# The stacks of a fused attention and convolution kernel: six transfers in a row, or three pairs that wait for TensorE's progress

## The reference

```python
# layer 0: shifted-window attention (windows of 8 x 8, shift 4, 3 heads of 8), then a gated convolution
xn  = layernorm(x over channels);  xw = windows(roll(xn, -4, -4))
q, k, v = split(xw @ qkv_w.T + qkv_b)
attn = softmax(q * hd**-0.5 @ k.T + bias + mask);  out = attn @ v @ proj_w.T + proj_b
x = x + roll(unwindow(out), 4, 4)
y = layernorm(x over channels, tokens in order).reshape(B, C, H, W)   # token rows read back as channel planes
y = conv3x3_depthwise(pin_w @ y)                                     # 24 -> 126 channels
x = x + pout_w @ (gelu(y[:, :63]) * y[:, 63:])
# layer 1: h = bn(w1 x); h = [h, max over even shifts of h - roll(h)]; gelu, two 1x1 products, residual, MLP
```

## Time and profile before

| what | value |
|---|---|
| three runs | 231.26 us median, 230.91 to 235.5 |
| profiled execution | 230.8 us, of which the span from first to last instruction is 228.9 |
| mean granted TensorE clock | 0.993 |
| busy share of the span | PE 92%, DVE 70%, ACT 60%, POOL 56% |
| transfers on SyncE's and the other hardware queue | 23.16 MB, 33.6% of 16 engines' span |
| instruction packets on queue q8 | 29, 0.48 MB |
| landing of store_y's 144 KB transfers, median | 2.3 us from issue |

### The profile page before, as it was taken

The page is one execution under the profiler, slowest core; times in us unless marked ns, Lnnn a source line. Parts: engine busy times, 40 slices in busy tenths (PEclk is TensorE's granted clock), DMA queues, the critical chain, the costliest instruction groups (busy, mean ns, idle before and its releaser), DMA issues.

```text
span 228.9 us, 8584 instructions
## 1 busy us (share of the span) xinstructions
PE 210.9 (92%) x3634; PEld 109.6 (48%) x3634; DVE 159.3 (70%) x284; ACT 137.0 (60%) x226; POOL 127.1 (56%) x165
## 2 busy tenths in 40 slices
PE   7779899999999999997799999999999987999980
PEld 4346666676757667665455444443333311222240
DVE  4677969698997989798755756344368789655332
ACT  3567676777859686763236333333346774898980
POOL 8245948466988869695989993223320000245433
PEclk9999999999999999999999999999999999999997
DMA  6950000120130464665637367777400001243312
GB/s 159 307 148 3 3 3 9 37 72 3 39 74 22 106 228 132 200 215 160 196 84 253 113 244 183 232 235 271 153 4 0 4 0 33 64 114 94 82 37 69
DMA packets 12541, 25.09 MB, mean 110 GB/s; under 512 B 6618, under 2 KB 8162, under 8 KB 10775
## 3 DMA queue, kind: packets, MB, share of 16 engines
q1 hardware_dynamic: 11606, 23.16, 33.6%
q0 software_dynamic: 896, 1.38, 2.7%
HBM read 18.63 MB, written 3.15 MB: 95 GB/s over the span
## 4 chain that ended last, share of the span: by engine, by line
PE 82%; DVE 7%; issue 4%; POOL 2%; ACT 2%; DMA 1%; POOLq 0%; DVEq 0%
PE psum L668 13%; PE psum L669 12%; PE psum L613 10%; PE psum L624 7%; PE psum L642 7%; PE psum L859 4%; PE psum L659 4%; PE psum L573 3%; PE psum L839 3%; PE psum L569 3%; PE psum L817 3%; PE psum L830 2%; PE psum L596 2%; PE psum L580 2%; PE psum L588 2%
## 5 line engine op out<-in xcount | busy, mean ns | idle before, releaser
L505 POOL TENSOR_TENSOR diff<-biased,mx 128x768 f32<-128x768 f32 x31 | 45.7, 1475 | 22.7 <-DVE mx L1146 22.7
L1277 DVE TENSOR_TENSOR gated<-psum,gel 64x512 f32<-64x512 f32 x32 | 22.1, 693 | 24.5 <-ACT gel L1030 24.5
L324 POOL DMA_DIRECT2D out<-yo x28 | 14.2, 515 | 44.2 <-DVE yo L1379 44.2
L1142 DVE TENSOR_TENSOR biased<-psum,pk 128x768 f32<-128x768 f32 x31 | 29.5, 952 | 11.2 <-PE psum L613 10.9
L1030 ACT ACTIVATE gel<-psum 64x512 f32<-64x512 f32 x32 | 18.9, 591 | 30.7 <-PE psum L669 30.6
L954 ACT ACTIVATE pt<-psum 128x768 f32<-128x768 f32 x32 | 25.9, 810 | 16.6 <-PE psum L624 16.4
L668 PE MATMUL psum<-sta,pk 108*128 108x512 f32 x64 | 33.7, 608 | 0.5 <-issue 0.5
L669 PE MATMUL psum<-stb,pk 108*128 108x512 f32 x64 | 32.7, 592 | 0.0
L1146 DVE TENSOR_REDUCE mx<-biased 128x12 f32<-128x768 f32 x31 | 29.5, 953 | 1.1
L613 PE MATMUL psum<-kmv,stq 32*64 32x192 f32 x512 | 28.1, 334 | 0.4 <-DVE biased L1154 0.3
L642 PEld LDWEIGHTS psum<-val,pt 128*32 128x32 f32 x1536 | 17.1, 110 | 12.4 <-issue 12.2
(11 more groups left out here) (108 smaller groups left out, 343.9 us busy)
## 6 DMA issues: line engine op xcount, KB each, us to landing
sta<-scratch SPq DMA_DIRECT2D x24, 288.0 KB
stb<-scratch SPq DMA_DIRECT2D x24, 288.0 KB
xtok<-xt SPq DMA_DIRECT2D x8, 192.0 KB, 4.2
xin<-xw SPq DMA_DIRECT2D x8, 192.0 KB, 5.5
x<-x1s SPq DMA_DIRECT2D x28, 48.0 KB
out<-yo POOLq DMA_DIRECT2D x28, 48.0 KB, 2.0
pk<-pack SPq DMA_DIRECT2D x1, 827.5 KB, 7.1
scratch<-ytok SPq DMA_DIRECT2D x4, 192.0 KB, 3.9
```

What stands on the lines that cost most here:

```text
L505: g.tensor_tensor(diff[:, t % 2].rearrange("q g w n -> q (g w) n"), scores_of, mx[:, t % 2].unsqueeze(2).to_broadcast([128, 4 * NH, WT]), ...
L1142: v.tensor_tensor(biased[:, slot].rearrange("q (p s) -> q p s", p=2), banks, wt("rpb").unsqueeze(1).to_broadcast([128, 2, 2 * NH * WT]), A ...
L1277: v.tensor_tensor(gated[64 * (b % 2):64 * (b % 2) + 64, b // 2, c * CH:(c + 1) * CH], bank(u % 4)[64:128], gel[:, u % 4, :], ALU.mult).the ...
```

## The change

load_stack takes a semaphore and two counts in place of the flag that was always off. Its first two transfers go out at once; the third (y = 2 of sta) waits until the semaphore has reached the first count, and with it goes the fourth; the fifth waits for the second count, and with it goes the sixth. For image 0 and image 1's first half the semaphore is mixed, behind them conv_made. Image 2's first half waits for 8 and 9 there, its second half and image 3 for 10 and 10.

```diff
-        def load_stack(queue, b, h, paced=False):
+        def load_stack(queue, b, h, progress, second, third):
...
-                    if paced and (n or y):
-                        at, before = divmod(3 * n + y - 1, 3)
-                        queue.wait_ge(stack_in[at][b][h], 16 * (before + 1))
+                    if 3 * n + y == 2:
+                        queue.wait_ge(progress, second)
+                    if 3 * n + y == 4:
+                        queue.wait_ge(progress, third)
...
-                    load_stack(sp, b, 0, False)
-                if m in (5, 7):
-                    load_stack(sp, m // 2 - 2, 1, False)
+                    load_stack(sp, b, 0, mixed, *((21, 22) if m == 4 else (29, 30)))
+                if m == 5:
+                    load_stack(sp, 0, 1, mixed, 26, 27)
+                if m == 7:
+                    load_stack(sp, 1, 1, conv_made, 3, 4)
             store_y(sp, 5)
             wait_for_y(2)
             sp.wait_ge(scores_made, 4 * NCH)
-            load_stack(sp, 2, 0)
+            load_stack(sp, 2, 0, conv_made, 8, 9)
...
-            load_stack(sp, 2, 1)
+            load_stack(sp, 2, 1, conv_made, 10, 10)
...
-            load_stack(sp, 3, 0)
+            load_stack(sp, 3, 0, conv_made, 10, 10)
             sp.wait_ge(conv_made, NCH)
-            load_stack(sp, 3, 1)
+            load_stack(sp, 3, 1, conv_made, 10, 10)
```

## The result

The changed kernel took 236.75 us (median of four runs, 235.94 to 237.26), the kernel before 231.08 beside it (229.17 to 235.5). The ratio is 1.0256, with a 95% interval from 1.0197 to 1.0314: slower, by about 5.9 us; whether by more than two per cent, of which the prediction speaks, the interval leaves open. Forecast were 233.6 in 230.4 to 236.0, so the direction was right and the time lies 0.75 us above the range. The profiled execution took 236.44 us with a span of 234.6 (230.8 and 228.9 before), and the mean granted clock is 0.983 against 0.993.

A forecast was written before the change was run, and what follows sets the result against it. TensorE's work bounds until about 153, then SyncE's list. Late masks put convolution 24 +2.0 us; with the clock's 1.5 it starts at 163.5 against 160.9, +2.6: 233.4, plus 0.2 gives 233.6, range 230.4 to 236.0.

The forecast's parts named there:

- two per cent, of which the prediction speaks: Whole kernel: 4.6 us, about what a measurement tells from no change; chances faster 0.01, slower 0.09, within 0.90.
- SyncE is 2.1 us later: SyncE's list at image 1's second half: starts at 119.63 instead of 117.55, and the lateness goes on undiminished.
- My bound of +3.5: Upper bound on SyncE's lateness, if image 1's first half takes the 6.2 us that it took before.
- The 1.0 us that the prediction gives these waits: Image 1's second half, waits on conv_made 3 and 4: nothing, or 1.0 us if TensorE is not 2.9 us ahead.
- The second part of the size is the clock: Behind TensorE's 4.5 us stand before convolution 20: clock falls to 0.50, costing 1.5 us, bounded by nothing and 2.9.
- If both gaps close, it reaches convolution 20 at 150.6.: TensorE comes 2.91 us sooner than 153.53, then stands 4.5 us until masks at 155.1.
- the two gaps: TensorE stops in mixes at 103.35 (1.56 us) and 109.33 (1.35), read as running dry of instructions; worth 2.91 us.
- the first rival, the sooner landing: store_y(5) lands 2.3 us after issue, not 6.3, making everything behind 1.9 us sooner; 228.5 to 230.3, chance 0.10.
- Image 0's first half: SyncE's list free some 3 us later at about 89.3; nothing waits there, the next wait swallows the delay.
- "Nothing" for the waits on conv_made: Image 1's second half and image 2: waits over when the list reaches them, so nothing added if TensorE is ahead.
- The slip of residual(7): VectorE's residual(7) needs store_x1(5), issued until 119.6; a slip costs TensorE up to 1 us, taken from its later stand.
- The second rival: Gaps stay or move: 1.56 us stays in mix 27, SyncE 3.7 us late; 234.4 to 236, chance 0.13.

The follow-up runs named there:

- 1: Changed kernel with only the waits of image 0's second half (mixes 26 and 27) kept; 235.32 us, ratio 1.0185 to the kernel before.
- 6: 4 with the waits on conv_made left out, so waits in image 0 alone; 231.5 us, ratio 0.9928 to the kernel before.
- 15: Changed kernel with only the waits on mixes 26 and 27, behind store_y(3) and store_x1(4), and store_y(5) ahead of image 1's second half; 230.21 us, 0.996.
- 4: Changed kernel with store_y(3) and store_x1(4) ahead of image 0's last two second-half pairs, no waits on mixes 29 and 30; 233.76 us, ratio 1.0076.
- 10: Changed kernel with only the waits on conv_made, none on mixed; 234.73 us, ratio 1.0228 to the kernel before.
- 11: Changed kernel with only the waits of image 0's first half (mixes 21 and 22); 231.93 us, ratio 1.0113 to the kernel before.
- 5: Changed kernel plus five extra 512-column multiplications on TensorE ahead of convolution 20; 234.90 us, ratio 1.0111 to the kernel before.
- 12: Changed kernel run once more, nothing altered; 232.73, 236.23, 236.55 and 236.64 us.
- 14: Changed kernel as it is, run beside 13 on one chip; 235.87 us, ratio 1.0207 to the kernel before.
- 3: Changed kernel plus ten extra 512-column multiplications on TensorE ahead of convolution 20; 238.93 us, ratio 1.0319 to the kernel before.
- 8: Kernel before, without added waits, with store_y(5) moved ahead of image 1's second half; 230.83 us, ratio 0.9949.
- 2: Changed kernel with all added waits but those of image 0's second half (mixes 26 and 27); 238.82 us, ratio 1.0302 to the kernel before.
- 13: Changed kernel plus four extra multiplications (3.4 us) on TensorE ahead of convolution 20; 234.43 us, ratio 1.0161 to the kernel before.

## Why the prediction was wrong, point by point

**The mechanism was the one forecast.** The waits of image 0's second half hold SyncE's list, nothing behind absorbs it, TensorE's stand moves to convolution 20, and the clock falls there. Kernels 1, 6 and 15 show it from both sides: two waits alone bring three quarters of the loss, and with the same waits listed behind the stores it is gone. In the three profiles with a late list, nothing added to TensorE and the clock up behind the stand (4, 10, 11), image 2's first half is 2.13, 1.69 and 0.48 us late, and the execution 2.0, 2.1 and 0.5 us longer than that of the kernel before.

**The step that failed is "SyncE is 2.1 us later", the list's term, in its size.** It was 3.95 in the profile. The 1.87 us between come from single pieces: the third pair went out at 104.00, not 103.45 (+0.55: the mix ended at 103.98 instead of 103.38, behind a gap of 0.53 that has appeared at 99.38 in TensorE's list, and SyncE followed after 0.02, not the 0.07 that the sum has); store_y(3) took 1.26 with its pause, not 0.42 (+0.84); store_y(4) 2.42, not 2.01 (+0.41, one issue of 1.17); the rest 0.07. I used for each piece its own row of the trace before and replaced the one long issue in them by the normal row. But both parts of the sum change from one execution to the next. Issues of one to two microseconds come again and again, at other places: from the end of the third pair to image 1's second half the list took 14.73 us in 5, 15.17 in 12, 15.34 in 14, 15.97 in the profile after, 16.16 in 1 and 16.60 in 3, where the sum has 14.60. And the list inherits whatever time TensorE has lost by mix 27: the third pair was out at 104.84 in 14 and at 106.49 in 3, where the sum has 105.03. Together the list was 2.11 us late in 5, 2.63 in 14, 3.95 and 4.01 in the profile after and in 12, and 5.54 in 3. My bound of +3.5 took one long stack for all of them.

**Nor would 2.1 us have lasted.** The sum has TensorE 2.9 us ahead at the waits on conv_made; it was 0.95 ahead at convolution 0. A list near the forecast is then held next by convolution 3: with image 1's second half at 119.66 and 120.18, store_y(5) still went out 3.2 (5) and 3.1 us late (14). The 1.0 us that the prediction gives these waits if TensorE is not ahead is also too little by the chain of the kernel before, where convolution 3 ends at 124.28 + 0.86 = 125.14:

```profile
124.28 0.86 PE psum L669 x2
```

The last pair, two issues of 0.79, would be out at 126.7, 2.3 us after the 124.4 of the sum.

**The second part of the size is the clock:** 2.05 us against the 1.5 taken, inside the bounds; it was 2.9 in 1 and 1.6 in 14. The upper bound came from a row that can't carry it. The granted clock recorded beside the eight matmuls at the kernel's start is 1.00, not 0.50 (window, us, PE busy, clock, DMA share, GB/s; the kernel before), so that their 5.49 us are no price of the lower level:

```profile
3.00:5.00 2.00, 2.00 (x4) 1.00 1.04 266
```

That 2.9 was a good upper bound all the same is luck.

**Why the range failed too.** At convolution 20 the time was 157.75 against 155.1 forecast, +2.65: 1.74 of the list (3.82 late at image 2's second half against 2.08), 0.8 of a stack that landed later still, 0.11 of start. With 0.55 of the clock that is the 3.2 us by which the time missed. Both upper ends stood in the text, but they were not taken together: 153.0 + 3.5 + 6.87 + 2.9 = 166.3, or +5.4 and about 236.4; even that has no term for the stack's later landing. They are not independent either: a later list makes a longer stand, and the clock was down over convolution 20 after stands of 3.10 (1), 4.50 (12) and 4.67 us (the profile after), and up after 1.66 (4), 2.06 (10) and 2.82 (14).

**"If both gaps close, it reaches convolution 20 at 150.6."** Both were gone, and TensorE reached it at 153.08 (before 153.53). Of the 2.91 us, 0.95 were left at convolution 0 (111.81 against 112.76) and 0.45 here; the rest went at the wait for residual(7), below. PE's timeline of the changed kernel shows what came next:

```profile
99.91 0.61 PE L655 MATMUL psum<-pk,ot 128*96 128x128 f32 x4 [0.53 <-issue]
...
106.17 0.59 PE L627 MATMUL psum<-pk,diff 64*128 64x64 f32 x12 [0.32 <-POOL diff L508]
107.10 0.88 PE L616 MATMUL psum<-kmv,stq 32*64 32x192 f32 x16 [0.35 <-DVE biased L1145]
...
109.64 0.59 PE L627 MATMUL psum<-pk,diff 64*128 64x64 f32 x12 [0.47 <-POOL diff L508]
110.66 0.64 PE L655 MATMUL psum<-pk,ot 128*96 128x128 f32 x4 [0.43 <-DVE ot L1176]
```

I read the two gaps as 2.91 us of TensorE's time. POOL and VectorE, both in the chain of each step, were next late after about one: the four waits for them and the new gap of 0.53 are 2.10 us. Nor is the closing of both gaps the change's alone: in 8 and 10, without an added wait in attention, the gap of 1.35 at 109.33 is gone too, and in 10 TensorE comes to convolution 0 at 112.16, 0.60 us ahead. That the stand came out at 4.67 against the 4.5 forecast is an accident: TensorE came 2.5 later than forecast, and the masks 2.5 later as well.

**What held:** store_y(5) landed 6.3 us after its issue (126.27 to 132.55), so the first rival, the sooner landing, fell. Its mechanism exists: the landing took 4.6 us in 2, 4.4 in 4 and 4.1 in 10, where the waits on conv_made hold the stack ahead apart, and 2.9 in 15, where the store stands ahead of the stack. **Image 0's first half** cost 0.5 us in the profile of 11. **"Nothing" for the waits on conv_made** held in the changed kernel, where the list arrives late, and is wrong as a property of those waits (4, 5, 10). **The slip of residual(7)** came as named: it waited for store_x1(5), which is the chain's 2.54 us of transfer at 120.75, and TensorE for it 0.26.

**The second rival** had nearly the right list, 3.7 us late, by a mechanism that was not there: mix 27 ran through in 0.56. It was near by its number only. The page "Runtime: NRT & Kernel Launch" of the Trainium skill, section "Instruction fetch mechanics", calls the crossing of an instruction block "mostly hidden"; kernel 2 shows a crossing that cost 2.53 us with six transfers ahead of it, kernel 11 one at the same place that cost at most 0.3 with the same six, and kernels 6 and 15 show all crossings between 84 and 113 us hidden, with the same transfers spread.

**What stays open.** How much of the time is the clock's: the rows give 2.05 us in the profile after, 2.9 in 1 and 1.6 in 14 (convolution 24 there took from 163.98 to 167.33, 3.35 us instead of 1.72), the medians of 13 and 14 a difference of 1.4 that isn't significant. Why single issues on SyncE take one to two microseconds, and why the stop in mix 27 comes in one execution and not in another: no run here was made to tell.

## What to carry to other kernels

A wait put into a list that works strictly in order is paid by all that is queued behind it: before adding one, follow the list to the next transfer that an engine stands waiting for, count the idle time in between, and list unrelated stores ahead of the wait. A list that waits for another engine also inherits that engine's lateness, which a sum of the list's own rows leaves out. Several waits in one list don't add at the same step; the one that ends last counts, so taking one away may show nothing, and one that looks free may only be covered by another. When two bounds come from the same lateness, such as a late stack and a clock that falls in the stand before it, the range has to hold both ends at once.

## What the runs showed of the hardware

- Issues by SyncE are uneven: 0.38 or 0.51 us for store_y's transfers, and 1.17 to 1.50 for single ones of the same kind and size in 1 and in the changed kernel. The same stretch of one list, from the third pair of image 0's second half to image 1's second half, took 14.73 us in one profile and 16.60 in another (5 and 3).
- The stop at the instruction block in mix 27 was 1.56 us before, 2.53 in 2, 2.42 in 8 and 1.16 in 10, each with all six transfers in a row ahead of it, but at most 0.3 in 11, also with six in a row; in the twelve profiles with the transfers spread it was at most 0.51 (13).
- The granted clock stayed at 1.00 over convolution 20 after stands of 1.66 (4), 2.06 (10) and 2.82 us (14), and was at 0.50 after 3.10 (1), 4.50 (12) and 4.67 us (the changed kernel). The length of the stand alone doesn't decide: before convolution 24 the clock fell after 1.66 us in 14 and after 1.96 in 2, and stayed up after 1.05 in 4. In the changed kernel it fell 1.8 us after TensorE's last matmul and came back 4.0 us after the first new one.
